# A two-layer attention and feed-forward kernel: inverses of the softmax sums taken a group later, V projections spread over other chunks, third bf16 parts on the Pool engine, late weights loaded inside group 0

## The reference

```python
# 1. attention a: 32 heads of 8, biases, softmax(q k / sqrt(8)) v, then @ Wo + bo
# 2. ffn
h = silu(x @ w_gate) * (x @ w_up)        # 256 -> 1024
h = keep the 2 largest |h| of each 4     # 2:4 sparsity
y = h @ w_down                           # 1024 -> 256
# 3. attention b: 32 query heads, 8 key/value heads, no bias; scores of
#    keys j with i-128 <= j < i get -1e10 before the softmax; then @ wo
# 4. the same ffn again, same weights
```

## Time and profile before

| | |
|---|---|
| Median of 3 runs | 1737.73 us (1736.84 to 1738.2) |
| Profiled execution | 1737.54 us, its span 1735.8 us, granted clock 0.976 |
| PE busy | 1665.3 us, 96% |
| DVE busy | 1481.5 us, 85% |
| ACT busy | 1281.4 us, 74% |
| POOL busy | 250.9 us, 14% |
| Chain that ended last | PE 86%, DMA 5%, DVE 4%, ACT 2%, issue 2%, SPq 1% |

### The profile page before, as it was taken

One profiled execution on the slowest core, in us unless ns is written; L12 is line 12 of the kernel. 1 busy time (PEld: TensorE's weight loads), 2 busy tenths in 40 slices (PEclk: granted clock), 3 DMA queues, 4 the chain that ended last, 5 costly groups with the idle time before them and its releaser, 6 DMA issues.

```text
span 1735.8 us, 39249 instructions
## 1 busy us (share of the span) xinstructions
PE 1665.3 (96%) x13872; PEld 656.4 (38%) x13872; DVE 1481.5 (85%) x2158; ACT 1281.4 (74%) x2424; POOL 250.9 (14%) x609
## 2 busy tenths in 40 slices
PE   6789999999899999999997999999998999999999
PEld 3312222222222223777653222222222222247777
DVE  6989999999799993676677999999998999936655
ACT  3269999999799998333222999999998999973221
POOL 1220000000000000000000322333322233310000
PEclk9879999999899999999997999999999999999999
DMA  6853443333443312200403322223322222111000
GB/s 179 263 141 67 85 80 60 66 64 61 78 86 69 65 35 62 61 1 0 112 14 118 69 58 49 55 49 71 67 54 49 52 51 56 40 55 49 13 12 25
DMA packets 72124, 114.67 MB, mean 66 GB/s; under 512 B 12464, under 2 KB 27824, under 8 KB 71984
## 3 DMA queue, kind: packets, MB, share of 16 engines
q1 hardware_dynamic: 71984, 112.63, 28.5%
HBM read 71.96 MB, written 40.63 MB: 65 GB/s over the span
## 4 chain that ended last, share of the span: by engine, by line
PE 86%; DMA 5%; DVE 4%; ACT 2%; issue 2%; SPq 1%; POOL 0%; POOLq 0%; DVEq 0%; ACTq 0%
PE psum L723 30%; PE psum L705 19%; PE psum L781 13%; PE psum L675 12%; PE psum L801 6%; DMA max_rows<-mT 4%; PE psum L640 2%; PE psum L761 2%; PE psum L659 1%; DVE mneg L1187 1%; DMA area<-max_rows 1%; ACT area L962 1%; DVE xn L1193 1%; PE psum L693 1%; PE psum L622 1%
## 5 line engine op out<-in xcount | busy, mean ns | idle before, releaser
L962 ACT ACTIVATE area<-psum 128x512 f32<-128x512 f32 x2048 | 1097.7, 601 | 67.8 <-PE psum L705 41.3
L705 PE MATMUL psum<-area 51*128 51x512 bf16 x2048 | 643.7, 388 | 20.3 <-DMA area<-max_rows 18.0
L723 PE MATMUL psum<-area 128*32 128x256 f32 x8192 | 658.8, 394 | 0.6 <-POOL area L1428 0.4
L1193 DVE CUSTOM_DVE_ANT_0 xn<-psum,band 128x1024 f32<-128x1024 f32 x512 | 588.7, 1224 | 22.0 <-PE psum L675 21.3
L1187 DVE TENSOR_REDUCE mneg<-psum 128x1 f32<-128x1024 f32 x512 | 582.8, 1215 | 22.4 <-PE psum L675 22.2
L675 PE MATMUL psum<-area 48*128 48x512 bf16 x1024 | 306.2, 392 | 10.7 <-DVE mneg L1187 10.5
L723 PEld LDWEIGHTS psum<-area 128*32 128x32 f32 x8192 | 162.6, 108 | 404.2 <-issue 268.7
L705 PEld LDWEIGHTS psum<-area 51*128 51x128 bf16 x2048 | 142.5, 94 | 448.2 <-ACT area L962 358.2
L675 PE MATMUL psum<-k_max_b,area 48*128 48x512 bf16 x1024 | 295.1, 389 | 8.7 <-DVE mneg L1193 8.0
L1005 ACT ACTIVATE area<-psum 128x512 f32<-128x512 f32 x64 | 38.2, 597 | 158.8 <-PE psum L781 158.8
L1409 POOL TENSOR_TENSOR mparts<-mneg,nought 128x16 bf16<-128x16 f32 x64 | 14.1, 220 | 763.9 <-DVE mneg L1187 541.5
(11 more groups left out here) (70 smaller groups left out, 822.3 us busy)
## 6 DMA issues: line engine op xcount, KB each, us to landing
ctx_rows<-area SPq DMA_DIRECT2D x64, 256.0 KB, 3.4
area<-q_stacks SPq DMA_DIRECT2D x32, 384.0 KB, 7.3
area<-k_stacks SPq DMA_DIRECT2D x64, 192.0 KB, 5.7
area<-q_stacks_b SPq DMA_DIRECT2D x32, 384.0 KB, 5.7
area<-q_stacks SPq DMA_DIRECT2D x32, 192.0 KB, 4.4
area<-q_stacks_b SPq DMA_DIRECT2D x32, 192.0 KB, 3.2
area<-ctx_rows SPq DMA_DIRECT2D x16, 256.0 KB, 4.8
area<-inv_rows SPq DMA_DIRECT2D x16, 256.0 KB, 5.5
```

Source lines behind the costliest of these rows:

```text
L705: pe.matmul(psum[:, BANK_OF["exp", g, u, head], :], k_st[lo:lo + ROWS + PARTS, buf, 0 if a else head // 2, kt * P:(kt + 1) * P], q_st[lo:l ...
L723: mm = pe.matmul(psum[head * VW:(head + 1) * VW, BANK_OF["ctx", g, qh], cols], vaug[:, buf, kt, head, :], probs[:, u % PRING, head, cols], ...
L962: act.activation(probs[:, u % PRING, head, :], psum[:, BANK_OF["exp", like, u, head], :], ACT.Exp, scale=SCALE).then_inc(bank_freed, 1)
L1193: dve.tensor_tensor_reduce(band_out[:, c % 2, :], slot, band[:, at:at + SEQ], 1.0, -3.0e38, ALU.add, ALU.max, mneg[:, qh, col:col + 1]).th ...
```

## The change

There are four edits. (1) SP's `store_inverses` is cut in three. Reading the sums (`load_sums`) stays after group 8. Storing the inverses moves to the end of group 10. The wait for that store moves into `load_ctx`, near the end. DVE inverts after group 9's list, not after group 8's. (2) `load_late_weights` moves into SP's group 0 of attention a, behind the second `move_max`. (3) In attention a, six V pieces stand at chunks 1, 5, 17, 19, 21, 23, and the two early ones get PSUM banks 4 and 5, which spares them the wait for the transposed x; chunk 1 waits for their evacuation. In attention b, V of batch 1 comes in four parts of two tiles at chunks 19, 21, 23, 24. (4) The `low` of batch 1 goes from DVE to POOL in both attentions: 8 of them in a, 6 in b.

```diff
-        V_BANKS = [[(6, 7), (6, 7)], [(4, 4), (7, 7)]]
+        def v_bank(a, b, v):
+            if a:
+                return 7 if b else 4
+            return 4 + v if b == 0 and v < V_EARLY else 6 + v % 2
-        V_CHUNKS = [(1, 3, 9, 11, 13, 15), (CPH + 9,)]
+        V_CHUNKS = [(1, 5, CPH + 1, CPH + 3, CPH + 5, CPH + 7), (CPH + 3, CPH + 5, CPH + 7, CPH + 8)]
+        V_TILES = BT // len(V_CHUNKS[1])
 # SP
                 move_max(a, g, buf, 1)
+                if first and a == 0:
+                    load_late_weights()
                 store_ctx(a, g, 0)
                 if ahead >= 1:
                     move_max(a, g + 1, 1 - buf, 0)
+                if inverses is not None:
+                    store_inverses(a, inverses)
...
-                sp.wait_ge(inv_stored, 16 * (BATCH * a + b + 1))
-            def load_ctx(a, b):
+            def load_ctx(a, b):
+                sp.wait_ge(inv_stored, 16 * (BATCH * a + b + 1))
...
-                store_inverses(a, 0)
-                with sp.Fori(GPB // 2, (GROUPS - 4) // 2) as i:
+                load_sums(a, 0)
+                group(a, GPB + 1, 1)
+                group(a, GPB + 2, 0, inverses=0)
+                with sp.Fori(GPB // 2 + 1, (GROUPS - 4) // 2) as i:
 # PE, project_v and attend
                 elif b == 0 and v == 0:
                     pe.wait_ge(w_loaded[0], 32)
+                elif b == 0 and v == V_EARLY:
                     pe.wait_ge(ln_evac, 8)
...
+                    if a == 0 and c == 1:
+                        pe.wait_ge(v_done, V_EARLY)
                     if a == 0 and c == CPH + 3:
                         pe.wait_ge(rest_done, BATCH * PCH[a])
-                        pe.wait_ge(v_done, BATCH * VCH[a])
                         turn_max(a, 0, 0)
 # DVE
-                if i:
+                if i and b == 0:
                     low(a, b, i - 1)
...
+                group(a, GPB + 1)
                 invert_sums(a, 0)
-                with dve.Fori(GPB // 2, (GROUPS - 2) // 2) as i:
+                group(a, GPB + 2)
+                with dve.Fori(GPB // 2 + 1, (GROUPS - 2) // 2) as i:
 # POOL
+            def low(a, b, i):
...
+                pool.wait_ge(mid_done, n + 1)
+                pool.tensor_tensor(parts[SLOT[s]][0:rows, 2, half * BANK:(half + 1) * BANK],
+                                  resid[a][0:rows, n % 2, :],
+                                  parts[SLOT[s]][0:rows, 1, half * BANK:(half + 1) * BANK],
+                                  ALU.subtract).then_inc(lo_done, 1)
...
                 if a == 1:
+                    for i in range(HALF):
+                        low(a, 1, i)
                     split_max(a, 0, 0)
+                    for i in range(HALF, PCH[a]):
+                        low(a, 1, i)
+                if a == 0:
+                    for i in range(PCH[a]):
+                        low(a, 1, i)
                 extend_v(a, 0, 0)
```

More of the change, by code:

```diff
@@ L518, in store_ctx, with group @@
                 sp.dma_start(ctx_rows[a][g, :, :, qh * BANK:(qh + 1) * BANK], ctx_sb[:, qh, :]).then_inc(ctx_stored, 16)
-            def group(a, g, buf, first=False, ahead=2):
+            def group(a, g, buf, first=False, ahead=2, inverses=None):
                 if ahead >= 1:
@@ L535, in stored_all, with load_sums @@
                     sp.wait_ge(stacks_stored[i], stored(i, n))
-            def store_inverses(a, b):
+            def load_sums(a, b):
                 sp.dma_start(sums[:, b, :],
@@ L541, in store_inverses @@
                                  "g i (s c) -> g i s c", c=2 * P)).then_inc(sums_loaded, 16)
+            def store_inverses(a, b):
                 sp.wait_ge(isums_ready, BATCH * a + b + 1)
@@ L575, in _ @@
                     move_max(a, 0, 0, 0)
-                if a == 0:
-                    load_late_weights()
                 stored_all(a, BATCH)
@@ L595, in _ @@
                 sp.wait_ge(ctx_stored, 16 * HALF * GROUPS * (a + 1))
+                load_sums(a, 1)
                 store_inverses(a, 1)
@@ L643, in project_half, with project_v @@
                 mm.then_inc(proj_ready, 1)
-            def project_v(a, b, v):
+            def project_v(a, b, v, tiles=None):
                 if a == 1:
@@ L655, in project_v @@
                     pe.wait_ge(v_done, n - 1)
-                for t in range(per):
+                for t in tiles or range(per):
                     tok = b * SEQ + (v * per + t) * P
                     for k in range(DK):
-                        mm = pe.matmul(psum[:, V_BANKS[a][b][v % 2], t * width:(t + 1) * width], xnT[:, k, tok:tok + P],
+                        mm = pe.matmul(psum[:, v_bank(a, b, v), t * width:(t + 1) * width], xnT[:, k, tok:tok + P],
                                        w_a[a][2][:, k, :], start=(k == 0), stop=(k == DK - 1))
-                mm.then_inc(v_ready, 1)
+                if not tiles or tiles[-1] == per - 1:
+                    mm.then_inc(v_ready, 1)
             def max_scores(a, g, buf, c):
@@ L823, in attend @@
                     if c in V_CHUNKS[a]:
-                        v = (0 if a else V_EARLY) + V_CHUNKS[a].index(c)
-                        project_v(a, 1 if a else v // VCH[0], v % VCH[a])
+                        v = V_CHUNKS[a].index(c)
+                        if a:
+                            project_v(a, 1, 0, tiles=range(V_TILES * v, V_TILES * (v + 1)))
+                        else:
+                            project_v(a, *divmod(V_EARLY + v, VCH[0]))
+                    if a == 0 and c == 1:
+                        pe.wait_ge(v_done, V_EARLY)
                     if a == 0 and c == CPH + 3:
                         pe.wait_ge(rest_done, BATCH * PCH[a])
-                        pe.wait_ge(v_done, BATCH * VCH[a])
                         turn_max(a, 0, 0)
@@ L1128, in copy_v @@
                 dve.wait_ge(v_ready, VBASE[a] + b * VCH[a] + v + 1)
-                bank = psum[:, V_BANKS[a][b][v % 2], :]
+                bank = psum[:, v_bank(a, b, v), :]
                 if a == 0:
@@ L1294, in attend @@
                         split_step(a, 1, P_FIRST[a] + (c - P_CHUNKS[a][0]) // 2)
-                    if c - 1 in V_CHUNKS[a]:
-                        v = (0 if a else V_EARLY) + V_CHUNKS[a].index(c - 1)
-                        copy_v(a, 1 if a else v // VCH[0], v % VCH[a])
+                    if a and c - 1 == V_CHUNKS[a][-1]:
+                        copy_v(a, 1, 0)
+                    if a == 0 and c - 1 in V_CHUNKS[a]:
+                        copy_v(a, *divmod(V_EARLY + V_CHUNKS[a].index(c - 1), VCH[0]))
                 group(a, 0)
@@ L1395, in extend_v @@
                 pool.tensor_copy(vaug[:, buf, :, :, 0:HD], src).then_inc(vaug_ready, 1)
+            def low(a, b, i):
+                j, half = ORDER[a][i]
+                w, m, rows = QUARTERS[a][j]
+                n, s = PBASE[a] + b * PCH[a] + i, QBASE[a] + b * NQ[a] + j
+                pool.wait_ge(mid_done, n + 1)
[3 more added lines that the diff above has]
+                                  ALU.subtract).then_inc(lo_done, 1)
             def split_max(a, g, qh):
```

## The result

The changed kernel took 1707.88 us (median of 4 runs, 1706.65 to 1708.38) against 1737.97 us for the kernel before (median of 4 in the same set): ratio 0.9822, 95% interval 0.9802 to 0.9842. The forecast was 1705.6 us, faster. The profiled execution took 1707.96 us with a span of 1706.0 us, against 1737.54 and 1735.8.

The account below looks back on a forecast made before the run. PE, DVE and ACT, each over 95% busy, share one pace, so stalls are lost for good. Gains of 7.1 + 5.2 + 16.8 + 3.0 = 32.1 us gave 1705.6 us; forecast band 1702 to 1709 (50%), wider range 1698 to 1715.

Parts of the forecast that it names:

- Inverses: Group 9 of both attentions: SP no longer waits for DVE before the loads, saving 9.6 and 7.2 us, 16.8 in all.
- Late weights: Group 0 of attention a: weights go out behind the second half's maxima, removing PE's stall and half clock, 5.2 us.
- the room of 4 us: Group 0 of a: the weights are through about 4 us before the turn at unit 12 needs the DMA engines.
- First lead: Before group 0 of attention a: first score at 83.0 us instead of 90.13, gain 7.1 us, bounds 4 and 9.
- the DMA chain: First lead: batch 1's stores end at 79 us, maxima's rows are back at 82.9; the last chain to finish.
- VectorE's chain: First lead: chunks, `rest` and V evacuations take 36.6 us from 43.8, ending at 80.4; first score 81.2.
- POOL: A `low` of batch 1 in both leads takes 1.2 us, scaled from the bias's row of 8.81 us.
- The bound of 4.5 us: Leads: a `low` on POOL costs nothing up to about 4.5 us, as DVE waits for it only two projections later.
- rule of the shared port: DVE and GpSimd lock one port pair when DVE has two SBUF inputs; `rest` has one, so the sum stays unchanged.
- Second lead: Into group 0 of attention b: 3.0 us gained, with a stall of 2 to 5 us at unit 8; bounds 0 and 6.8.
- gain 3.7, less 0.7 for half clock after such a stall, for about one step: Second lead: unit 8 starts at 966.3 instead of 970.0 us, less some 0.9 us a step at half clock: 3.0.
- the bound of 6.8: Second lead's upper bound: DVE's chain puts the first score at 941.2 us, 6.8 us earlier.

Follow-up runs that it names:

- the leads alone: Kernel before with only the V pieces spread and the third parts (`low`) of batch 1 on POOL: 1730.66 us, ratio 0.9951.
- third parts three times over: Changed kernel with every third part (`low`) of batch 1 computed three times on POOL: 1717.33 us against 1708.17 in the same set.
- the stack's load moved: Changed kernel with the load of group 1 of a's maxima stack issued behind the first maximum rows, not between batch 1's stores: 1706.02 us.
- third parts on VectorE: Changed kernel with the third parts (`low`) of batch 1 back on VectorE, V pieces still spread: 1708.16 us, ratio 0.9814.

## Why the prediction was right

The forecast was 32.1 us off the span and the measured change 29.8. Every edit acted by the mechanism that was named. The closeness of the sum is in part luck: the first lead reached its number by another way than the one worked out, and the same instructions in the second lead gained 1.3 to 4.6 us in the four kernels and executions that have them without a further edit there.

**Inverses, 16.8 us forecast, 16.1 measured.** Right in mechanism: taking SP's wait away removed the late loads, the late rows, and the half clock. In attention a, 0.7 us remained as a short wait for the rows. The reciprocal costs its 1.1 us as before.

**Late weights, 5.2 forecast, 5.16 measured,** alone and in company. What I did not see is that this term and the leads' are not independent: with the leads alone the stall grew by 1.9 us. The weights took from 100.5 to about 114 us, 13.5 us and not the 10 of the prediction, so the room of 4 us that I gave them was hardly there. Nothing was late for it: the turn's rows went out at 114.78.

**First lead, 7.1 forecast, 7.27 measured.** The first score was forecast at 83.0 from the DMA chain and came at 84.01 from it. VectorE's chain was put at 81.2, and came at 82.6 once the DMA chain was out of the way. So the first score gained 6.1 us, not 7.1. The clock was back earlier, and from the first score to the turn at unit 4 it took 12.13 us instead of 13.28, which made up for the microsecond; the prediction had counted on nothing there.

**POOL, 1.2 us a `low` forecast, 1.15 measured;** scaling the bias's row held. The Trainium skill's 2.6 cycles an element for a two-input operation ("GPSIMD Engine Reference", section "3.1 Elementwise — side-by-side cycle accounting") would make an estimate of 1.11 us, and the measurement agrees. Its rule of the shared port ("SBUF — State Buffer", cited in the prediction) predicted no contention for a `rest` with one SBUF input, and the trace agrees: the slowest `rest` took 751 ns with POOL at work and 752 before. The bound of 4.5 us up to which I counted a slower one as free was wrong. It asked how late one third part may come, where all eight come one behind the other: what counts is the pair's 2.9 us, and tripled, at 3.59 us, `rest` waited for POOL and the first score was 6.0 us later.

**Second lead, 3.0 forecast, 1.26 measured: the mis-sized term.** The step was "gain 3.7, less 0.7 for half clock after such a stall, for about one step". The stall at unit 8 was foreseen at 2 to 5 us and was 2.60. The half clock lasted three steps of up to 0.87 us extra each, about 2.6 us, not 0.7: this is the term that failed. The step had also taken the late rows for a fact of the stores' chain. The rows were late for the loads issued just ahead of them, 6.9 us instead of 2.1; with the order turned the stretch gave 6.72 us, near the bound of 6.8 that I had set for no stall. With a shorter stall (the leads alone, 1.55 us) it gave 4.6 us, so the 1.26 us are the outcome of these executions and not of the edit alone.

## What to carry to other kernels

In an in-order DMA queue, ask of each small transfer that an engine waits for which bulk loads were issued just ahead of it, and whether they are needed sooner; turning the two round was worth 5 us here, and no later wait came of it. Price a wait of TensorE by the wait and by the steps at half clock that may follow it. An operation that is moved to another engine must fit, each time, into the pace of those that wait for it; how late a single one may be is not the bound. And when one stretch decides about an edit, look at it in every execution at hand: the third parts on POOL seemed to cost 3.1 us in the second lead, and the same instructions took 50.24 and 51.08 us in two other kernels where they took 53.56 here.

## What the runs showed of the hardware that was not expected

Waits of PE at unit 8 of group 0 of b of 2.49 and 2.60 us (two executions of the changed kernel) and of 4.28 us (third parts three times over) were each followed by about 7 us at half clock. Waits of 0.72, 0.73 and 1.55 us at the same place (the stack's load moved, third parts on VectorE, the leads alone) left the clock at 1.00. What lies between 1.55 and 2.49 us no run shows.

The same 12 KB, from issue to landing, took 2.1 us ahead of the loads, 6.4 to 7.7 us behind eight loads in six executions, and 9.1 us behind the stores of the first lead.
